# One write of a whole head's position scores in place of two writes of half a head

## The reference

```python
content_score = jnp.einsum('bhsp,bhtp->bhst', q + u, k)      # 16 heads of 16 features, 512 x 512 scores
pos_score = jnp.einsum('bhsp,htp->bhst', q + v, pos)
pos_score = _relative_shift(pos_score)                       # below
weights = jax.nn.softmax((content_score + pos_score) / sqrt(16), axis=-1)

def _relative_shift(x):                                      # x: b, h, s, s
    x = jnp.pad(x, ((0, 0), (0, 0), (0, 0), (1, 0)))         # a zero ahead of each row: s x (s+1)
    x = x.reshape(b, h, s + 1, s)                            # the same numbers read as (s+1) x s
    return x[:, :, 1:, :].reshape(b, h, s, s)
```

## Time and profile before

| | us |
|---|---|
| median of 3 runs | 4870.55 |
| lowest and highest | 4867.86, 4873.32 |
| the profiled execution | 4870.25 |
| its span, first instruction to last | 4868.3 |
| PE busy | 4764.4 (98%) |
| DVE busy | 3686.6 (76%) |
| ACT busy | 3460.6 (71%) |
| POOL busy | 1710.5 (35%) |

### The profile page before, as it was taken

How to read it: one execution, slowest core, us unless ns; L and a number is a source line. 1 busy time by engine, 2 the same in 40 slices (tenths; PEclk the granted TensorE clock), 3 DMA queues, 4 the chain that set the end, 5 groups by cost and what they waited for, 6 DMA issues and landing times. The chain is left out here.

```text
span 4868.3 us, 111786 instructions
## 1 busy us (share of the span) xinstructions
PE 4764.4 (98%) x42412; PEld 3658.5 (75%) x42412; DVE 3686.6 (76%) x8040; ACT 3460.6 (71%) x5180; POOL 1710.5 (35%) x1545
## 2 busy tenths in 40 slices
PE   7899999999999999999999999989999999999997
PEld 3477777777777777777777777769999999999997
DVE  7699999999999999999999989963555555533344
ACT  3689989999998998999889999954333333344454
POOL 0222322222232222223222222224656565644443
PEclk9899999999999999999999999999999999999999
DMA  9899999999999999999999999973545555433259
GB/s 353 323 369 366 369 372 366 370 370 367 370 367 371 363 373 367 373 357 378 367 370 370 368 370 366 365 280 83 127 116 136 132 120 134 105 62 84 45 154 317
DMA packets 394026, 1389.58 MB, mean 285 GB/s; under 512 B 51104, under 2 KB 128800, under 8 KB 327712
## 3 DMA queue, kind: packets, MB, share of 16 engines
q1 hardware_dynamic: 270624, 778.39, 44.0%
q0 software_dynamic: 122880, 604.05, 38.7%
HBM read 708.00 MB, written 674.23 MB: 284 GB/s over the span
## 5 line engine op out<-in xcount | busy, mean ns | idle before, releaser
L735 DVE CUSTOM_DVE_ANT_0 att_shifted<-att_quad,att_shifted 128x512 f32<-128x512 f32 x2048 | 1324.1, 684 | 88.7 <-PE att_quad L977 88.4
L599 ACT ACTIVATE att_shifted<-att_shifted,att_mn 128x512 f32<-128x512 f32 x2048 | 1360.6, 717 | 0.3 <-DVE att_mn L735 0.3
L594 ACT ACTIVATE ring<-att_quad 128x1024 f32<-128x1024 f32 x1024 | 1047.8, 1023 | 308.6 <-PE att_quad L965 308.4
L998 PE MATMUL att_tp<-ident,att_shifted 128*128 128x128 f32 x8192 | 1122.5, 280 | 6.1 <-DVE att_pt L745 5.3
L745 DVE COPY att_pt<-att_tp 128x512 f32<-128x512 f32 x1536 | 1011.0, 686 | 128.9 <-PE att_tp L998 121.3
L998 PEld LDWEIGHTS att_tp<-ident,att_shifted 128*128 128x128 f32 x8192 | 878.8, 141 | 301.6 <-issue 175.2
L1461 DVE TENSOR_TENSOR ffn_hp<-ring,ffn_hp 128x512 fp32r<-128x512 f32 x512 | 477.7, 933 | 685.8 <-ACT ring L1398 662.6
L485 POOL DMA_DIRECT2D att_shifted<-xs_d x512 | 279.3, 545 | 2038.0 <-DMA xs_d<-ring 1691.7
L1396 ACT ACTIVATE ffn_hp<-ffn_up 128x512 fp32r<-128x512 f32 x512 | 305.9, 597 | 915.0 <-PE ffn_up L1542 899.8
L965 PE MATMUL att_quad<-att_pos,att_qv 64*128 64x512 f32 x2048 | 832.3, 447 | 12.0 <-ACT ring L594 11.9
L1503 PE MATMUL ffn_yp<-ffn_w2p,ffn_hp 128*128 128x256 f32 x6144 | 827.7, 284 | 3.4 <-DVE ffn_hp L1461 1.7
(11 more groups left out here) (111 smaller groups left out, 4694.5 us busy)
## 6 DMA issues: line engine op xcount, KB each, us to landing
xs_d<-ring SPq DMA_DIRECT2D x1024, 513.0 KB, 8.2
att_shifted<-xs_d POOLq DMA_DIRECT2D x512, 1024.0 KB, 9.3
att_shifted<-in_L_attn_x_dram SPq DMA_DIRECT2D x32, 512.0 KB, 7.0
xn_d<-att_shifted SPq DMA_DIRECT2D x32, 512.0 KB, 6.4
xt_d<-att_shifted SPq DMA_DIRECT2D x32, 512.0 KB, 7.6
gathered<-xt_d SPq DMA_DIRECT2D x32, 512.0 KB, 11.0
att_d<-att_osb SPq DMA_DIRECT2D x512, 32.0 KB
ring<-in_L_ffn_w_dram SPq DMA_DIRECT2D x16, 1024.0 KB
```

The lines of the kernel that those rows point to most:

```text
L594: act.activation(xo[:, kk % NW, 2 * half:2 * half + 2, 1:S + 1], xp[:, :, :], ACT.Copy).then_inc(x_out, 1)
L599: act.activation(shifted[:, kk % NX, t], shifted[:, kk % NX, t], ACT.Exp, bias=mn[:, kk % NX, t:t + 1], scale=-1.0).then_inc(exp_done, 1)
L735: dve.tensor_tensor_reduce(out=shifted[:, kk % NX, t], in0=sp_[:, t % 2], in1=shifted[:, kk % NX, t], scale=-0.25, scalar=-NEG, op0=ALU.ad ...
L998: ins = pe.transpose(tp[:, c % 2, t * P:(t + 1) * P], shifted[:, kk % NX, t, c * P:(c + 1) * P], ident[:, :])
```

## The change

`write_x` waits once, until both halves of the head are put out, and issues one transfer of 513.0 x 2 KB with one completion. The three waits on `x_written` count 16 a head in place of 32. The reading, the buffers, the slots and the order of all other work are as they were.

```diff
-                    for half in range(2):
-                        rows = slice(2 * half, 2 * half + 2)
-                        wait_alone(sp, x_out, (i * BH + kk) * 2 + half + 1)
-                        sp.dma_start(xs_d[slot].rearrange("(p t c) -> p t c", t=TT, c=S + 1)[:, rows], xo[:, kk % NW, rows]).then_inc(x_written[slot], 16)
+                    wait_alone(sp, x_out, (i * BH + kk) * 2 + 2)
+                    sp.dma_start(xs_d[slot].rearrange("(p t c) -> p t c", t=TT, c=S + 1), xo[:, kk % NW]).then_inc(x_written[slot], 16)
...
-                                sp.wait_ge(x_written[k], B * H // NX * 32)
+                                sp.wait_ge(x_written[k], B * H // NX * 16)
...
-                    wait_alone(pool, x_written[slot], (i * (BH // NX) + turn + 1) * 32)
+                    wait_alone(pool, x_written[slot], (i * (BH // NX) + turn + 1) * 16)
...
-                        act.wait_ge(x_written[slot], (i * (BH // NX) + turn + 1) * 32)
+                        act.wait_ge(x_written[slot], (i * (BH // NX) + turn + 1) * 16)
```

## The result

The changed kernel is slower. Its median was 4890.88 us (4884.33 to 4902.80, 11 runs) beside 4874.18 for the kernel before (11 runs on the same chips): a ratio of 1.0034, with 1.0025 to 1.0043 as its 95% interval, 17 us. Run again later, beside a fresh set of runs of the kernel before (e8), it stood at 1.0018 (1.0010 to 1.0027). 4871 had been forecast, and a range of 4862 to 4888. All ratios leave out one execution of e10, which ran at a granted clock of 0.596 and took 7036.54 us.

The account below looks back on a forecast made before the run. The prediction took TensorE's queue, 5.91 us a head, as the bound, with no compute engine late because of transfers. It summed 4870.25 + 1 for rare late heads + 0 for the rest = 4871 us, range 4862 to 4888.

Parts of the forecast that it names:

- 1 for rare late heads: VectorE's waits for the reading: 1 head in 100 late by 0.5 us, 2.6 us, taken as nearer 1 us.
- The sign of being wrong: At L735, VectorE's first addition of a head: waits for `att_shifted<-xs_d` of over 10 us in sum would refute the forecast.
- waits are the slack of a prefetch, not a stall: GpSimd's waits for the write, 1374.7 us in 2500, make no compute engine late; GpSimd is busy 28%.
- The 4.7 us: Usual slack between a head's second half and its first addition: 22.7 us, less 18.0 for write, GpSimd and reading.
- The argument that the first half's bytes are still queued behind the head before: Write queue: holding the first half back loses little, so the write lands only +0.5 us later.
- the stated bound: Write's later landing after the second copy: at least 0, at most the whole 2.5 us between the halves.
- The 1.2 us: Write landing by the skill's formula: a megabyte issued at the second copy lands 1.2 us later than half a megabyte.
- The bound of +1.5: Reading's landing, sharing engines with larger write packets: +0.5 us allowed, between 0 and +1.5.
- the slower rival: Late writes stall VectorE's first addition: 4880 to 4900 or 4905 to 4955 us, decisive from about +2 us; chance 0.17.
- SyncE's saved issues: SyncE's queue: 512 issues of 0.32 us fewer, 164 us, worth 0 because nobody waits for them.
- The faster rival: Fewer, larger packets relieve the DMA engines: at most about 10 us, 4861; chance 0.07 of faster by over 0.2%.
- The third rival: Larger write piece is cut again into the old packets: 4871 again; chance 0.76 together with the forecast.

Follow-up runs that it names:

- e8: Changed kernel, unedited, run again beside a fresh set of runs of the kernel before: 1.0018 of the kernel before.
- e10: Kernel before with both half writes held until the second half is put out, plus a third part of the query buffer `qn`: 1.0004 of the kernel before.
- the held halves: Kernel before, its two half writes kept but neither issued until the second half is put out: 1.0065 (e1) and 1.0049 (e9).
- e14: Kernel before with only a third part of the query buffer `qn` added, as a control: 0.9996 of the kernel before.
- e1: Kernel before, both half writes still sent separately but neither issued until the second half is put out: 4899.42 us, 1.0065.
- e9: Same kernel as e1, two half writes held until the second is put out, run again in a later set: 1.0049 of the kernel before.
- e11: Changed kernel (one merged write) with a third part of the query buffer `qn`: 1.0019 of the kernel before.
- e6: Kernel before, each head's reading issued as two transfers in pieces of 4096 bytes in place of one in 8192: 0.9999 of the kernel before.
- e2: Changed kernel, eight unused numbers between the halves in SBUF, so its one write moves in 256 pieces of 4104 bytes: 1.0901 of the kernel before.
- e7: Kernel before, a spare number behind each buffer row, so each half write moves in 256 pieces of 2052 bytes: 1.1948 of the kernel before.
- e3: Changed kernel with position scores put out six heads ahead in place of five: 1.0402 of the kernel before.
- e5: Kernel before, with position scores put out six heads ahead in place of five: 1.0407 of the kernel before.

## Why the prediction was wrong

**The step that failed** is the sum's one term that was not nothing, "1 for rare late heads": 1 head in 100, late by 0.5 us. The changed kernel had 18 late heads in 512, by 1.1 us each, 19.6 us in sum, and 12 heads with 10.0 us in e8. What was mis-sized ahead of it is the delay, +1.9 us and not +1.0: in the trace of before, 2 of the 317 heads have under 1.0 us of slack, which is the forecast's 1 in 100, and 10 have under 1.9, which is 16 in 512. A second way, through GpSimd's queue, was put at nothing; it is shown for the held halves, and its share in the changed kernel stays open. The sign of being wrong that the prediction named, over 10 us of waits for `att_shifted<-xs_d`, came in the first profile; in e8 they stood at 10.0.

**What bounds the kernel.** VectorE waited for no reading before, and TensorE set the pace, as said. But GpSimd's "waits are the slack of a prefetch, not a stall" left out what stands behind the wait in the same queue. In the trace of before the splits there still waited for TensorE, 78.7 and 41.6 us; in e1 that had shrunk to 6.8 and 10.5. This was a slack to count, and the trace of before showed the path already: ScalarE's 1.4 us ahead of L558, which are gone in e14. e1, e9 and e10 show its price: 1.0049 to 1.0065 with it, 1.0004 without.

**The slack.** The 4.7 us were right as a mean (4.6). The sum took 8.3 us for the write, the median of all halves, where the second half took 8.6, which changes little. The count of tight heads above could have been read from the trace of before ahead of the run. It shows how fast the number of late heads rises with the delay: fivefold from 1.0 to 1.9 us.

**The write.** Forecast +0.5 us on its landing; measured +1.1 on the second half (e1, e9 and e10 held back: +1.2 to +1.5). The argument that the first half's bytes are still queued behind the head before holds in part: of the 2.8 us that lie between the halves on average, two fifths were lost. The middle of the stated bound, 1.25, would have been nearly right. The 1.2 us that the prediction took from the Trainium skill, "DMA: Bandwidth & Descriptors", section "Anatomy of one DMA — SWDGE (gpsimd) path", is near this. But that section is on transfers that GpSimd issues, and these writes are SyncE's. And the held halves land as late with no megabyte in one transfer, so the size of the transfer is not what set it.

**The reading.** Forecast +0.5, measured +0.8. The bound of +1.5 held it. The sum of +1.9 is just at the point "from about +2 us in all" from which the slower rival was said to decide. That rival named VectorE's stall, which happened, and its lowest price, "about 30 us at most", 4880 to 4900, takes in the measured 4890.88. It had a chance of 0.17. Its working was not borne out as well: it took a tenth of the heads to be late by 0.6 us, where 18 were, by 1.1.

**What cost nothing.** SyncE's saved issues, the wait for the buffers, the end of the phase: as forecast, no wait of these shows in the changed profile.

**The faster rival** said that larger packets relieve the DMA engines. That does not show. The write queue moved its bytes a little faster, 470.51 MB in 48.9% of 16 x 2500 us, 24.1 GB/s an engine in place of 23.4, and the readings' queue as much slower, 441.17 MB in 51.3%, 21.5 in place of 22.4. The DMA share stayed at 1.01.

**The third rival**, that the piece would be cut again, was wrong: over the span q1 has 73,728 packets fewer (270,624 before, 196,896 now). That is 65,536 for the pieces, as forecast, and 8,192 for the completions, 16 a transfer.

Open is the split of the changed kernel's 0.2 to 0.3% between the two ways. ScalarE's 6 us plead for a small part of the second. Taking it away (e11) was worth nothing against one measurement of the changed kernel and 0.15% against the other.

## What to carry to other kernels

Merging two transfers takes the head start from the first, and in a chain of transfers that head start is slack; before merging, compare it with the slack that is left in the tightest heads, not with the mean. When a wait grows, look at what stands behind it in the same queue: an engine that is busy 28% of the time can still hold up the others. And in two pairs of runs here, the size of the pieces on one queue changed how soon the transfers of the other landed.

## What the runs showed of the hardware

- With both queues loaded, halving the readings' pieces made the writes land 1.5 us sooner (8.6 to 7.1) and the readings 0.5 us later (9.4 to 9.9; e6). The bytes moved were the same.
- Writing two pieces a partition in place of one, at the same piece size of 4104 bytes, took the write queue from 23.4 to 18.9 GB/s an engine (e2); four of 2052 bytes a partition and head, in two transfers, to 16.1 (e7).
- Two matmuls of 64 rows each started at the same time where they lay in different halves of the array (2001.89 twice), and 0.2 to 0.3 us apart in the same half (e3). A head took 5.91 us with an odd distance, and 6.3 with an even one (397 readings in 2500 us, e5).
- With two issues back to back, the last half of a head landed 10.3 to 10.6 us after the copy (e1, e9, e10); one transfer of the same bytes landed after 9.8 to 10.0 (changed, e8, e11).
